# Moving a few on-chip tiles by 128 bytes, so that all matmul operands start at an odd multiple of 128

## The chip, the cores and the metric

The kernel runs on one core of one Trainium2 chip. The metric is the device time of one execution in microseconds (us). Three runs of the kernel before took 561.51, 562.34 and 562.51; the median is 562.34.

## The reference

Eight batches of 256 rows and 1024 features, in float32. Cross attention over a context of the same size, then a linear layer with 4-bit weights, both with a layer norm ahead and a residual behind:

```
def _L0_xattn_ref(text, features, Wq, bq, Wk, bk):
    Q = einsum('btx,dx->btd', text, Wq) + bq
    K = einsum('bpx,dx->bpd', features, Wk) + bk
    scores = einsum('btd,bpd->btp', Q, K) / sqrt(1024)
    attn = softmax(scores, axis=-1)
    return einsum('btp,bpd->btd', attn, features)

def _L0_ffn_ref(x, qweight, qzeros, scales, bias, g_idx):
    zeros = 4-bit fields of qzeros, + 1
    w = 4-bit fields of qweight
    wbin = where(w > 0, 1, -1)
    weights = scales[g_idx] * (wbin - zeros[g_idx])
    return x @ weights + bias

x = x + _L0_xattn_ref(layernorm(x), ctx, Wq, bq, Wk, bk)
x = x + _L0_ffn_ref(layernorm(x), qweight, qzeros, scales, bias, g_idx)
```

## The kernel before

The kernel keeps float32 accuracy with a fast matmul type: each operand is split into a high part (a rounded copy, made by ScalarE) and a low part (what is left, made by VectorE or GpSimd), and each product is three matmuls into the same accumulator: high by high, high by low, low by high. The helper is `three` (lines 1234 to 1237); in a matmul the first operand is the stationary one (128x128, loaded as weights) and the second the moving one (512 columns, in the scores 256). Line 1235 is high by high, 1236 has the low moving operand, 1237 the low stationary operand.

There are four stages on TensorE, in this order.

1. Projection (`proj`, lines 1262 to 1289). M = Wq' Wk, a 1024x1024 matrix, so that the scores are x M ctx'. Stationary wq_hi, wq_lo; moving wk_hi (line 1279), wk_lo (1282), wk_hi again with wq_lo (1285). 64 blocks (b, c) of two halves of three matmuls, 384 in all. The transposes of the first x tiles stand between the last blocks.
2. t products (lines 1340 to 1362). t = M' x' in four pairs of batches: for each pair p and each column block j, 24 matmuls (8 row blocks i by three), stationary m_hi and m_lo, moving xT_hi and xT_lo. 32 groups, 768 matmuls. The groups are counted n = 8p + j. After some of them stand gather steps (`gather`, two matmuls each, lines 1320 and 1321), which look up the scales and zeros of the 4-bit weights; VectorE makes the weights from them (`pick`, `weights`), and a layer norm and transposes of the next x run beside them.
3. Scores and attention products, batch by batch (`scores`, `pv`). The scores of one batch are 48 matmuls of 256 columns, stationary tT_hi and tT_lo, moving cT_hi and cT_lo. The attention product is 24 matmuls of 512 columns, stationary pT, moving cn.
4. The linear layer (`product`), as a seven-product scheme over halves: for each of eight batches (a pass) seven products a11, a12, s2, s1, s3, s4, a22 of 12 matmuls each (4 blocks k by three). Stationary l_hi and l_lo, moving r_tile0 to 2 for k = 0 to 2 and r_last for k = 3.

The order on each engine is written out by hand, with semaphores between engines. Tiles lie at places that are written out too: `at(name, kb, ...)` puts a tile at the byte `16512 + kb * 1024` of every partition (lines 76 to 79). Places are reused from stage to stage. Those that the change touches:

- WKL (line 102) holds wk_lo in stage 1 and xT_lo in stage 2, 32 KB from 98.125.
- tT_hi0, tT_hi1 (line 159) at 98.125 and 106.125; tT_hi2, used for batch 0 alone, is at 194.25.
- slot 6 and 7 (line 125), 8 KB each from 114.125: the t results and tT_lo of batches 6 and 7, the residual rows xres6 and xres7, and the unpacked weights and right sums of blocks 1 and 2 or 0 to 2.
- r_last2 (line 169), moving operand of the last two products' last block (s4 and a22), at 106.125.
- l_hi and l_lo of s2 and s1 (lines 178 to 180) at 98.125 and 102.125, the low part 2 KB behind the high.

16512 is 129 times 128. All other tiles of large matmuls are at whole KB or at a quarter of one, and so begin at an odd multiple of 128 bytes; those in the list begin at an even multiple.

Of the kernel before, what the change touches and what calls it, by code (L numbers as in the profile page):

```python
# [9 lines left out]
F32R = mybir.dt.float32r  # L10
# [3 lines left out]
P = 128  # L14
HALF = 512
# [33 lines left out]
def xattn_ffn_kernel(nc, x, ctx, Wq, bq, Wk, bk, qweight, qzeros, scales, bias, g_idx, out):  # L49
    B, S, D = x.shape  # L50
    G = scales.shape[0]
    assert ctx.shape == x.shape and S == 2 * P and D == 2 * HALF and bq.shape[0] == D
    NB = D // P
# [17 lines left out]
    with ExitStack() as stack:  # L71
# [6 lines left out]
        def at(name, kb, shape, dt):  # L78
            return nc.alloc_sbuf_tensor_at(name, shape, dt, offset=BASE + int(kb * KB)).ap()
# [19 lines left out]

        m_hi = at("m_hi", 2, [P, NB, D], F32R)  # L100
        m_lo = at("m_lo", 34, [P, NB, D], F32R)
        WKL = 98.125
        wk_hi = at("wk_hi", 66, [P, NB, D], F32R)
        wk_lo = at("wk_lo", WKL, [P, NB, D], F32R)

# [16 lines left out]
        xT_hi = at("xT_hi", 66, [P, NB, 2 * S], F32R)  # L122
        xT_lo = at("xT_lo", WKL, [P, NB, 2 * S], F32R)

        slot = [kb + 8 * i for kb in (130.25, 146.25, 82, 114.125) for i in range(2)]
        t_pair = [at(f"t_pair{p}", slot[2 * p], [P, 2, NB, S], F32) for p in range(PAIRS)]


# [21 lines left out]
        s3 = at("s3", 188.25, [P, D], BF16)  # L150
# [5 lines left out]
        cn_lo = at("cn_lo", 186.25, [P, QT, D], F32R)  # L156
        cT_hi = [at(f"cT_hi{i}", kb, [P, NB, S], F32R) for i, kb in enumerate((178.25, 66))]
        cT_lo = [at(f"cT_lo{i}", kb, [P, NB, S], F32R) for i, kb in enumerate((186.25, 74))]
        tT_hi = [at(f"tT_hi{i}", kb, [P, NB, S], F32R) for i, kb in enumerate((98.125, 106.125, 194.25))]
        tT_lo = [at(f"tT_lo{b}", slot[b], [P, NB, S], F32R) for b in range(B)]  # L160
        cin = [at(f"cin{i}", kb, [P, QT, D], F32) for i, kb in enumerate((162.25, 170.25, 58))]
        xres = [at(f"xres{b}", slot[b], [P, QT, D], F32) for b in range(B)]
# [3 lines left out]


        r_tile = [at(f"r_tile{k}", kb, [P, 2 * N_PROD, HALF], F32R) for k, kb in enumerate((2, 30, slot[0]))]
        r_last = [at(f"r_last{i}", kb, [P, m, HALF], F32R) for i, (kb, m) in enumerate(((slot[0] + 28, 2), (66, 8), (106.125, 4)))]

        def right(k, m):
            if k < KH - 1:
# [2 lines left out]
            return r_last[i][:, m - first, :]  # L175


        l_place = dict(a11=162.25, a12=166.25, s2=98.125, s1=102.125, s4=170.25, s3=174.25, a22=178.25)
        l_hi = {n: at(f"l_hi_{n}", kb, [P, HALF], F32R) for n, kb in l_place.items()}
        l_lo = {n: at(f"l_lo_{n}", kb + 2, [P, HALF], F32R) for n, kb in l_place.items()}  # L180
        l_sum = {n: at(f"l_sum_{n}", l_place[n] + 2, [P, HALF], F32) for n in ("s1", "s2", "s3", "s4")}
# [1311 lines left out]
```

## Time and profile before

| | us |
|---|---|
| median of three runs | 562.34 |
| profiled execution | 563.15 |
| its span | 561.4 |
| TensorE busy | 553.5 (99%) |
| VectorE busy | 386.2 (69%) |
| ScalarE busy | 240.4 (43%) |
| GpSimd busy | 186.2 (33%) |

The profile is of one execution. The span is from the first to the last instruction; 1.8 us of the execution lie around it. TensorE's weight loads are a row of their own and overlap its matmuls. A matmul's duration in the profile is the time from its start to its end, and the next one starts before that end.

### The profile page before, as it was taken

To read this page: it belongs to the slowest core of one execution; us is meant where nothing else is said; L and a number is where in the kernel's file an instruction comes from. 1 tells how busy PE (TensorE), PEld (TensorE's weight loads), DVE (VectorE), ACT (ScalarE), POOL (GpSimd) and SP (SyncE) were. 2 spreads that over 40 slices of the span, in tenths; PEclk is the share of its full clock that TensorE was granted. 3 is DMA by queue.
4 is the path that set the end of the run, shared out by engine and by line. 5 is a ranking of instruction groups with operands and counts; after the bars stand their busy time and mean duration, and the time that the engine had idled before them with its cause. 6 is when DMAs were issued, how large, how long until landed. Compare 5 with 4: busy or idle time off the path is not lost.

```text
span 561.4 us, 7445 instructions
## 1 busy us (share of the span) xinstructions
PE 553.5 (99%) x2702; PEld 456.5 (81%) x2702; DVE 386.2 (69%) x643; ACT 240.4 (43%) x426; POOL 186.2 (33%) x143
## 2 busy tenths in 40 slices
PE   7999999999999999999999999999999999999997
PEld 5888888887777877877889999999788888888886
DVE  4976765689889997785213555574877788778742
ACT  6964354301522342242336766676473253234110
POOL 2072000000000000000115977776667545743630
PEclk9999999999999999999999999999999999999999
DMA  8852100249576844743436699997517776773411
GB/s 287 252 156 70 37 1 0 90 172 311 177 224 238 251 188 150 223 160 131 156 99 245 231 340 354 313 402 308 228 76 224 226 218 231 216 233 110 118 75 75
DMA packets 47187, 106.59 MB, mean 190 GB/s; under 512 B 3576, under 2 KB 24064, under 8 KB 44976
## 3 DMA queue, kind: packets, MB, share of 16 engines
q1 hardware_dynamic: 40624, 99.84, 50.6%
q10 hardware_dynamic: 6528, 6.29, 5.0%
q8 instruction: 21, 0.34, 0.3%
q14 instruction: 14, 0.11, 0.1%
HBM read 66.27 MB, written 39.85 MB: 189 GB/s over the span
## 4 chain that ended last, share of the span: by engine, by line
PE 86%; DVE 5%; ACT 4%; DMA 2%; issue 2%; POOL 1%; SPq 0%; ACTq 0%; DVEq 0%; POOLq 0%
PE bank L1235 22%; PE bank L1237 22%; PE bank L1236 21%; PE bank L1279 5%; PE bank L1282 5%; PE bank L1285 5%; PE bank L1337 2%; DMA right_scratch<-part_hi 1%; DMA wk_stage<-in_L_xattn_Wk 1%; ACT yin L789 1%; POOL cn_lo L537 1%; PE bank L1245 1%; ACT cn_hi L586 1%; PE bank L1320 1%; DVE junk L1001 0%
## 5 line engine op out<-in xcount | busy, mean ns | idle before, releaser
L1235 PE MATMUL bank<-xT_hi,m_hi 128*128 128x512 f32 x256 | 104.5, 408 | 0.2 <-DVE xT_lo L853 0.2
L1237 PE MATMUL bank<-xT_hi,m_lo 128*128 128x512 f32 x256 | 100.8, 394 | 0.0
L1236 PE MATMUL bank<-xT_lo,m_hi 128*128 128x512 f32 x256 | 100.6, 393 | 0.0
L745 ACT ACTIVATE t_pair<-bank,ucol 128x512 f32<-128x512 f32 x32 | 22.0, 687 | 110.1 <-PE bank L1237 110.0
L1187 DVE TENSOR_TENSOR xres<-xres,bank 128x512 f32<-128x512 f32 x56 | 38.2, 682 | 36.9 <-PE bank L1237 36.8
L544 POOL TENSOR_TENSOR tT_lo<-t_pair,tT_hi 128x1024 fp32r<-128x1024 f32 x16 | 38.2, 2403 | 76.5 <-ACT tT_hi L586 76.5
L523 POOL TENSOR_TENSOR pairs<-mv,pairs 128x2 f32<-128x2 f32 x8 | 5.5, 693 | 164.4 <-DVE mv L920 164.4
L558 POOL TENSOR_TENSOR l_lo_s<-l_sum_s,l_hi_s 128x512 fp32r<-128x512 f32 x32 | 40.4, 1294 | 57.1 <-DVE l_sum_s L1128 57.1
L1235 PEld LDWEIGHTS bank<-xT_hi,m_hi 128*128 128x128 f32 x256 | 48.1, 188 | 13.1 <-DVE xT_lo L853 0.6
L1237 PEld LDWEIGHTS bank<-xT_hi,m_lo 128*128 128x128 f32 x256 | 48.1, 188 | 11.2
L1236 PEld LDWEIGHTS bank<-xT_lo,m_hi 128*128 128x128 f32 x256 | 48.2, 188 | 10.9 <-issue 0.2
L1279 PE MATMUL bank<-wk_hi,wq_hi 128*128 128x512 f32 x128 | 51.5, 403 | 1.5 <-ACT wk_hi L586 0.8
L1282 PE MATMUL bank<-wk_lo,wq_hi 128*128 128x512 f32 x128 | 50.7, 396 | 0.2 <-DVE wk_lo L862 0.2
L1285 PE MATMUL bank<-wk_hi,wq_lo 128*128 128x512 f32 x128 | 50.2, 392 | 0.0
L537 POOL TENSOR_TENSOR cn_lo<-cin,cn_hi 128x512 fp32r<-128x512 f32 x32 | 40.3, 1290 | 26.8 <-ACT cn_hi L586 26.8
L853 DVE TENSOR_TENSOR cT_lo<-bank,cT_hi 128x512 fp32r<-128x512 f32 x32 | 20.6, 686 | 34.1 <-ACT cT_hi L586 33.9
L564 POOL TENSOR_TENSOR xres<-xres,bias_rows 128x1024 f32<-128x1024 f32 x16 | 38.4, 2412 | 0.0
L1235 PE MATMUL bank<-r_tile,l_hi_s 128*128 128x512 f32 x96 | 37.7, 393 | 0.0
L1237 PE MATMUL bank<-r_tile,l_lo_s 128*128 128x512 f32 x96 | 37.7, 393 | 0.0
L1236 PE MATMUL bank<-r_tile,l_hi_s 128*128 128x512 f32 x96 | 37.7, 392 | 0.0
L1235 PE MATMUL bank<-cT_hi,tT_hi 128*128 128x256 f32 x128 | 37.0, 289 | 0.0
L1237 PE MATMUL bank<-cT_hi,tT_lo 128*128 128x256 f32 x128 | 36.1, 282 | 0.0
(148 smaller groups left out, 1257.2 us busy)
## 6 DMA issues: line engine op xcount, KB each, us to landing
cin<-in_ctx SPq DMA_DIRECT2D x8, 1024.0 KB, 5.5
xres<-in_x SPq DMA_DIRECT2D x8, 1024.0 KB, 11.2
out<-xres SPq DMA_DIRECT2D x15, 512.0 KB, 5.7
right_scratch<-part_hi SPq DMA_DIRECT2D x28, 256.0 KB, 2.2
xn_scratch<-xin SPq DMA_DIRECT2D x6, 1024.0 KB, 4.9
xq<-xn_scratch ACTq DMA_DIRECT2D x24, 256.0 KB, 5.5
r_tile<-right_scratch SPq DMA_DIRECT2D x6, 1024.0 KB, 11.0
yn_scratch<-yin SPq DMA_DIRECT2D x6, 1024.0 KB, 4.4
```

Of the source, the lines that this page charges most:

```text
L537: pool.tensor_tensor(cn_lo[:, kt, cols], cin[b % 3][:, kt, cols], cn_hi[:, kt, cols].bitcast(F32), ALU.subtract).then_inc(s_cnlo, 1)
L544: pool.tensor_tensor(tT_lo[b][:, ks, :], t_pair[b // 2][:, b % 2, ks, :], tT_hi[b % 2 if b else 2][:, ks, :].bitcast(F32), ALU.subtract).t ...
L558: pool.tensor_tensor(l_lo[name], l_sum[name], l_hi[name].bitcast(F32), ALU.subtract).then_inc(s_llo_p, 1)
L564: pool.tensor_tensor(x1_of(f)[:, t, :], x1_of(f)[:, t, :], bias_rows, ALU.add).then_inc(s_rb, 1)
L745: act.activation(t_pair[p][:, :, j, :], bank[n % 4][:, :].rearrange("p (b q) -> p b q", b=2), ACT.Identity, bias=ucol[:, j:j + 1]).then_in ...
L1187: dve.tensor_tensor(part, part, prod_bank(f, n)[:, :], ALU.add).then_inc(s_acc, 1)
L1235: pe.matmul(out_, a_hi, b_hi, start=start, stop=False, skip_group_check=True)
L1236: pe.matmul(out_, a_hi, b_lo, start=False, stop=False, skip_group_check=True)
L1237: return pe.matmul(out_, a_lo, b_hi, start=False, stop=stop, skip_group_check=True)
L1279: pe.matmul(out_, q_hi, wk_hi[:, c, cols], start=c == 0, stop=False, skip_group_check=True)
L1282: pe.matmul(out_, q_hi, wk_lo[:, c, cols], start=False, stop=False, skip_group_check=True)
L1285: ins = pe.matmul(out_, q_lo, wk_hi[:, c, cols], start=False, stop=c == NB - 1, skip_group_check=True)
```

## The change

Four numbers and what is built from them go down by 0.125 KB: 98.125 to 98, 102.125 to 102, 106.125 to 106 and 114.125 to 114. The tiles keep their sizes, and 128 bytes that lay free between 98 and 98.125 now lie free between the last moved tile and 130.25. No instruction is added, removed or moved on any engine.

```
-        WKL = 98.125
+        WKL = 98
...
-        slot = [kb + 8 * i for kb in (130.25, 146.25, 82, 114.125) for i in range(2)]
+        slot = [kb + 8 * i for kb in (130.25, 146.25, 82, 114) for i in range(2)]
...
-        tT_hi = [at(f"tT_hi{i}", kb, [P, NB, S], F32R) for i, kb in enumerate((98.125, 106.125, 194.25))]
+        tT_hi = [at(f"tT_hi{i}", kb, [P, NB, S], F32R) for i, kb in enumerate((98, 106, 194.25))]
...
-        r_last = [at(f"r_last{i}", kb, [P, m, HALF], F32R) for i, (kb, m) in enumerate(((slot[0] + 28, 2), (66, 8), (106.125, 4)))]
+        r_last = [at(f"r_last{i}", kb, [P, m, HALF], F32R) for i, (kb, m) in enumerate(((slot[0] + 28, 2), (66, 8), (106, 4)))]
...
-        l_place = dict(a11=162.25, a12=166.25, s2=98.125, s1=102.125, s4=170.25, s3=174.25, a22=178.25)
+        l_place = dict(a11=162.25, a12=166.25, s2=98, s1=102, s4=170.25, s3=174.25, a22=178.25)
```

## Rows read from the trace of the kernel before

**Rows 1.** Page, part 1: busy us (share of the span) and instructions, TensorE.
```profile
PE 553.5 (99%) x2702; PEld 456.5 (81%) x2702; DVE 386.2 (69%) x643; ACT 240.4 (43%) x426; POOL 186.2 (33%) x143
```
**Rows 2.** Windows: stretch, PE, PEld, DVE, ACT, POOL busy (x), clock, DMA, GB/s.
```profile
12.60:103.60 91.00, 91.00 (x418) 74.16 (x418) 66.24 (x92) 51.13 (x113) 14.61 (x10) 1.00 0.27 86
104.80:292.90 188.10, 187.47 (x818) 147.77 (x817) 139.83 (x259) 55.54 (x93) 8.94 (x8) 1.00 0.58 190
292.90:407.50 114.60, 113.78 (x764) 103.57 (x763) 63.32 (x109) 74.75 (x143) 81.77 (x54) 1.00 0.80 299
407.50:558.00 150.50, 150.50 (x665) 123.23 (x663) 109.90 (x176) 50.87 (x71) 77.01 (x57) 1.00 0.51 164
```
**Rows 3.** Timeline (start us, us, engine, line), last attention product: first and 24th matmul.
```profile
401.97 0.39 PE L1235 MATMUL bank<-cn_hi,pT_hi 128*128 128x512 f32 x1
...
407.18 0.40 PE L1237 MATMUL bank<-cn_hi,pT_lo 128*128 128x512 f32 x1
```
**Rows 4.** Timeline, projection: a matmul and the 48th behind it.
```profile
42.04 0.40 PE L1279 MATMUL bank<-wk_hi,wq_hi 128*128 128x512 f32 x1
...
53.24 0.40 PE L1279 MATMUL bank<-wk_hi,wq_hi 128*128 128x512 f32 x1
```
**Rows 5.** Timeline, t products: starts of neighbouring groups of 24, at three places.
```profile
110.77 0.40 PE L1235 MATMUL bank<-xT_hi,m_hi 128*128 128x512 f32 x1
...
116.37 0.40 PE L1235 MATMUL bank<-xT_hi,m_hi 128*128 128x512 f32 x1
...
187.25 0.39 PE L1235 MATMUL bank<-xT_hi,m_hi 128*128 128x512 f32 x1
...
192.74 0.39 PE L1235 MATMUL bank<-xT_hi,m_hi 128*128 128x512 f32 x1
...
263.40 0.40 PE L1235 MATMUL bank<-xT_hi,m_hi 128*128 128x512 f32 x1
...
268.95 0.40 PE L1235 MATMUL bank<-xT_hi,m_hi 128*128 128x512 f32 x1
```
**Rows 6.** Timeline, linear layer: starts of products a11, a12, s2, s3, s4, next a11.
```profile
461.56 0.39 PE L1235 MATMUL bank<-r_tile,l_hi_a 128*128 128x512 f32 x1
...
464.31 0.39 PE L1235 MATMUL bank<-r_tile,l_hi_a 128*128 128x512 f32 x1
...
467.04 0.40 PE L1235 MATMUL bank<-r_tile,l_hi_s 128*128 128x512 f32 x1
...
472.62 0.39 PE L1235 MATMUL bank<-r_tile,l_hi_s 128*128 128x512 f32 x1
...
475.36 0.39 PE L1235 MATMUL bank<-r_tile,l_hi_s 128*128 128x512 f32 x1
...
480.85 0.39 PE L1235 MATMUL bank<-r_tile,l_hi_a 128*128 128x512 f32 x1
```
**Rows 7.** Timeline, scores: 12 matmuls of batch 0, then 12 of batch 2.
```profile
294.41 0.28 PE L1235 MATMUL bank<-cT_hi,tT_hi 128*128 128x256 f32 x1
...
295.85 0.38 PE L1337 MATMUL bank<-ident,cin 128*128 128x128 f32 x2
...
315.11 0.28 PE L1235 MATMUL bank<-cT_hi,tT_hi 128*128 128x256 f32 x1
...
316.53 0.28 PE L1235 MATMUL bank<-cT_hi,tT_hi 128*128 128x256 f32 x1
```
**Rows 8.** Chain that ended last, 104 to 205: start us, us, what.
```profile
151.96 0.63 ACT xT_hi L586
...
181.31 0.39 PE bank L1320
...
202.72 0.50 PE bank L1235
```
**Rows 9.** DMA issues near 448 and 487: count, KB, us to landing.
```profile
xres<-x_scratch SPq DMA_DIRECT2D x1, 1024.0 KB, 4.8
...
xres<-x_scratch SPq DMA_DIRECT2D x1, 1024.0 KB, 4.6
```

## The prediction

> **What bounds the kernel now.** I read the busy shares first, then the stretches, then the starts of single matmuls in the timeline, and last the chain of waits. TensorE is busy 553.5 us of a 561.4 us span [rows 1], at full granted clock in all four stretches [rows 2], and in each it is busy for nearly the whole stretch: 91.00 of 91.00, 187.47 of 188.10, 113.78 of 114.60, 150.50 of 150.50 [rows 2]. So the end moves with the distance from the start of one matmul to the start of the next, which I call the step. The duration in a row (0.39 to 0.40) is no help: it is longer than the step, because matmuls overlap. The step must be taken from starts, over many matmuls, since a row is rounded to 0.01.
>
> **What the steps say.** The base is 16512 bytes, 129 times 128. A place in whole KB or with .25 behind it is therefore an odd multiple of 128, a place with .125 an even one. Only the places at 98.125 to 122.125 are even now. The change makes no instruction more or fewer and moves none; if it does anything, it does it through the step. Four comparisons:
>
> - The last attention product (rows of batch 7: cn and pT, all operands odd) starts its matmuls at 401.97 and its 24th at 407.18 [rows 3]: 5.21/23 = 0.2265, say 0.2267 with the half nanoseconds that rounding hides (12 matmuls are 2.72). This is my odd step.
> - The projection has wk_lo at an even place as the moving operand of every third matmul: 48 matmuls from 42.04 to 53.24 [rows 4], 11.20/48 = 0.2333.
> - The t products have xT_lo at an even place, also every third. One group of 24 takes 5.60 at the start (110.77 to 116.37), 5.49 in the middle (187.25 to 192.74), 5.55 late (263.40 to 268.95) [rows 5]: steps of 0.2333, 0.2288 and 0.2313. With the odd step it would be 5.44.
> - In the last stage, seven products of 12 matmuls, all in one pass of 19.29 (461.56 to 480.85) [rows 6]. a12, all odd, takes 2.73 (464.31 to 467.04). s2 and s1, whose stationary operands are at 98.125 and 102.125, take 5.58 for 24 (467.04 to 472.62), 2.79 each. s3 takes 2.74, and s4 and a22, three of whose twelve moving operands are at 106.125, 5.49 for 24 (475.36 to 480.85). a11, which follows such a product, takes 2.75.
>
> The last stage weighs most: same line, same shape, same engines beside it, and 2.79 against 2.73 goes with the place alone. It also shows that a product with every operand odd is still a little long just after a mixed one (2.74, 2.75) and then comes down to 2.73. The even operand need not be the moving one.
>
> **The change part by part.**
>
> 1. Projection (WKL, 98.125 to 98). 384 matmuls, 3 times 128. The first 18 wait for loads (until 12.6, the first stretch that isn't in rows 2), and what follows them gains; 366 x (0.2333 - 0.2267) = 2.4. Beside the x transposes of the last block a few steps are long for another reason; I take off 0.1: **2.3**.
> 2. t products (xT_lo, same place). 768 matmuls, 32 groups of 24, in which the two of each gather step are not counted. Seven groups go at 5.60 (five first, two last), three at 5.49, 22 at 5.55: 7 x 0.16 + 3 x 0.05 + 22 x 0.11 = 3.7. Not all of this reaches the end. The chain leaves TensorE for ScalarE at 151.96, goes on through VectorE's weights, sums, splits and row terms, and comes back at the gather at 181.31; and it comes back again at 202.72, when VectorE has made the last two blocks of xT_lo [rows 8]. Those stretches hang on work that isn't shortened. TensorE gets there earlier and waits: of the groups 8 to 12 I lose 5 x 0.11, of 16 and 17 0.05 + 0.11 (the gather near 210 is fed by the same unbroken run of VectorE), 0.7 in all. Left 3.0; I take **2.9**, since some other gather may come late too. Cover elsewhere: VectorE is busy 139.83 of 188.10 in this stage [rows 2], so it has room on the mean.
> 3. Scores (tT_hi at 98.125 and 106.125 for batches 1 to 7; tT_lo in the moved slots for 6 and 7). Here the rows go the other way. Batch 0, all odd, has 12 matmuls of 256 columns from 294.41 to 295.85, 1.44; batch 2, tT_hi even, has 12 from 315.11 to 316.53, 1.42 [rows 7]. Over 48 such matmuls in each of five batches (1 to 5) that would be 240/12 x 0.02 = 0.4; just behind the transposes both batches go alike, so I take half, **-0.2**. For 6 and 7 both are even now, and I put no loss.
> 4. Attention products. All their operands are odd before and after: 0.
> 5. Last stage (l_hi and l_lo of s1, s2; r_last of the last two products). 19.29 now, 84 x 0.2267 = 19.04 after: 0.25 a pass, 2.0 for eight; the first pass has waits in its first products, so **1.9**. VectorE has 109.90 of 150.50 busy [rows 2] and keeps up.
> 6. The other tiles at 114.125 (t_pair3, xres6 and xres7, some weights and sums of the right side). But for tT_lo they are no matmul's operand. What they might cost is in their transfers. The load of xres5 (at an odd place) takes 4.8 to land, that of xres7 (even now) 4.6 [rows 9], 1 MB each. If the place did that, it would cost 0.2 on a few loads that nothing waits for at their end: 0.
>
> The Trainium skill ("DMA: Bandwidth & Descriptors", How a descriptor splits into AXI transactions) speaks against the change here: a transfer whose start isn't at a multiple of 256 bytes fetches from the boundary below, so that a 4 KB row would cost 132 beats in place of 128. By that rule the moved loads would take 3% longer, an estimate of 0.14 on 4.7; by the rows a difference as small as this can neither be seen nor ruled out, and in the sum both give 0, because these loads are far ahead of their readers.
>
> Sum: 2.3 + 2.9 - 0.2 + 1.9 = **6.9 us**. The profiled execution took 563.15 in all, 1.8 of it around its span, and would take 556.2. It lies 0.8 above the median of the runs, 562.34; the gain set against that gives **555.4**.
>
> **Rivals.**
>
> A. The place is only half of it. For: the t products go at three rates with the same places, so the step also depends on how the reads stand to each other in time, and each rate holds for many groups until something disturbs it. An all-odd stage could settle at a rate such as 0.2288 [rows 5]. Against: every all-odd stretch of 512 columns comes down to 0.2267, after each disturbance. At 0.2288: projection 366 x 0.0045 = 1.6; t products 7 x 0.11 + 22 x 0.06 = 2.1, less 0.4 in VectorE's stretches, 1.7; last stage 1.9; scores -0.2. Gain 5.0, time 557.3.
>
> B. Nothing happens: 562.3. The steps would come from the kind of operand (split parts, tiles of another stage, other engines' reads) and not from its place. For: the projection's first matmul of three, with two odd operands, is as slow as the others. Against: a12 and s2 differ in nothing else that I can see, and neighbours of an even operand share its cost in the last stage too. The Trainium skill ("TensorE: Matmul & The Clock Gate", Step-by-step: what each phase is for) would have it so: matrix unit reads go through two independent ports, and loading the next weights takes no bandwidth from the running matmul. By it a place could not matter; the 2.79 against 2.73 of this trace is what it leaves unexplained.
>
> C. Slower. Two streams that start at the same parity get into each other's way, as the scores hint: 1.44 against 1.42 is 1.4%. If the all-odd step of the first two stages, where xT and m stand in other relations than r_tile and l_hi, went that way, 366 + 768 = 1,134 matmuls of some 0.233 would cost 1.4% more: +3.7, with the scores' 0.2 the time is 566.2. It decides where the mean step of those stages comes out above 0.2325. Against: the all-odd rows of 512 columns are the fastest in the trace.
>
> D. TensorE outruns VectorE in the whole t stage up to its last gather at 257: another 7 x 0.11 = 0.8 is lost, 556.2. This lies inside the range.
>
> **How the numbers follow.** The forecast, with D in it, 0.76; A 0.12; B 0.07; C 0.05. The likeliest case alone spans 554.2 (nothing lost to VectorE and in the scores, 2.4 + 3.7 + 2.0 gained) to 556.6. The range goes up to 557.8 to take in A and leaves B and C out, and down to 554.0. What a measurement of this kernel can tell from no change is 0.2%, 1.1 us. Faster: forecast, A, and none of the others, 0.88. Same: B and a little of A and C, 0.08. Slower 0.04.
>
> **What would show it.** Right: groups of 24 t matmuls of 5.44; 48 projection matmuls in 10.88; a pass of the last stage in 19.04, with s1 and s2 at 2.72; scores of batch 2 at 1.44 for 12; TensorE's wait for the gather near 181 about 0.5 longer than its 0.4. Wrong: steps as before (B), a rate between (A), a projection above 0.2333 (C), or more waits of TensorE on VectorE than 1 us (step 2).

## The result and the profile after

The changed kernel takes 556.12 us (median of four runs, 555.50 to 556.69), the kernel before 561.92 beside it (561.22 to 562.51). The ratio is 0.9897, with a 95% interval of 0.9879 to 0.9915: 5.8 us or 1.0% faster. Forecast were 555.4 and a range of 554.0 to 557.8.

The page of the changed kernel, part 1 (busy us, share of the span, instructions), answers to [rows 1]; the span is 554.9.

```profile
PE 546.3 (98%) x2702; PEld 456.5 (82%) x2702; DVE 385.4 (69%) x643; ACT 239.1 (43%) x426; POOL 186.1 (34%) x143
```

The same instructions, the same weight loads to the tenth of a microsecond, and 7 us less of matmul. The four stages as stretches of the changed kernel, cut as in [rows 2] (the projection from its 19th matmul, the last stage from product s2 of the first pass; columns as there):

```profile
12.80:102.60 89.80, 89.80 (x420) 74.54 (x419) 67.78 (x94) 52.03 (x115) 14.61 (x10) 1.00 0.29 90
102.60:288.00 185.40, 184.37 (x818) 147.77 (x817) 139.80 (x260) 54.97 (x92) 8.93 (x8) 1.00 0.59 193
288.00:402.80 114.80, 114.03 (x763) 103.81 (x762) 63.30 (x109) 74.68 (x143) 81.72 (x54) 1.00 0.79 298
402.80:551.30 148.50, 148.50 (x665) 123.14 (x664) 108.83 (x176) 50.45 (x71) 77.02 (x57) 1.00 0.51 165
```

Granted clock and instructions are as before; counts differ by one or two where a cut falls. Taken between the same instructions in both traces (the 19th projection matmul, the first t product, the first score, product s2 of the first pass, the last matmul), the stages are:

| stage | before | after | forecast | measured |
|---|---|---|---|---|
| projection behind its first 18 matmuls | 92.12 | 89.86 | -2.3 | -2.26 |
| t products | 188.13 | 185.32 | -2.9 | -2.81 |
| scores, attention, first two products of the last stage | 114.52 | 114.83 | +0.2 | +0.31 |
| last stage from s2 of the first pass | 150.34 | 148.43 | -1.9 | -1.91 |

The first loads came 0.18 later in the profiled run of after, so the spans differ by 6.5. The timeline of the changed kernel (start us, us, engine, line): first a projection matmul and the 48th behind it, which were 11.20 apart [rows 4], then one t group, which was 5.60, 5.49 or 5.55 [rows 5]:

```profile
41.38 0.39 PE L1279 MATMUL bank<-wk_hi,wq_hi 128*128 128x512 f32 x1
...
52.26 0.39 PE L1279 MATMUL bank<-wk_hi,wq_hi 128*128 128x512 f32 x1
...
114.00 0.39 PE L1235 MATMUL bank<-xT_hi,m_hi 128*128 128x512 f32 x1
...
119.44 0.39 PE L1235 MATMUL bank<-xT_hi,m_hi 128*128 128x512 f32 x1
```

10.88 and 5.44: the odd step, 0.2267, in both. The pass of the last stage that [rows 6] show, in the changed kernel: a11, s2, s3, and the next a11.

```profile
456.30 0.39 PE L1235 MATMUL bank<-r_tile,l_hi_a 128*128 128x512 f32 x1
...
461.74 0.39 PE L1235 MATMUL bank<-r_tile,l_hi_s 128*128 128x512 f32 x1
...
467.18 0.39 PE L1235 MATMUL bank<-r_tile,l_hi_s 128*128 128x512 f32 x1
...
475.34 0.39 PE L1235 MATMUL bank<-r_tile,l_hi_a 128*128 128x512 f32 x1
```

The pass is 19.04 (19.29 before), s2 and s1 together 5.44 (5.58). The scores went the other way. The starts of batch 2 and batch 3 in the kernel before, then in the changed one:

```profile
314.75 0.29 PE L1235 MATMUL bank<-cT_hi,tT_hi 128*128 128x256 f32 x1
...
328.10 0.29 PE L1235 MATMUL bank<-cT_hi,tT_hi 128*128 128x256 f32 x1
```

```profile
309.86 0.28 PE L1235 MATMUL bank<-cT_hi,tT_hi 128*128 128x256 f32 x1
...
323.28 0.28 PE L1235 MATMUL bank<-cT_hi,tT_hi 128*128 128x256 f32 x1
```

13.42 a batch, 13.35 to 13.37 before. And TensorE waits longer for VectorE, at the gather that [rows 8] have at 181.31 and at the last blocks of xT_lo (202.72 there). Before, then in the changed kernel; the brackets give TensorE's idle time and what ended it:

```profile
180.49 0.40 PE L1237 MATMUL bank<-xT_hi,m_lo 128*128 128x512 f32 x1
181.31 0.39 PE L1320 MATMUL bank<-zz,onehot 72*128 72x512 bf16 x1 [0.43 <-DVE wt L1030]
...
202.13 0.39 PE L1237 MATMUL bank<-xT_hi,m_lo 128*128 128x512 f32 x1
202.72 0.50 PE L1235 MATMUL bank<-xT_hi,m_hi 128*128 128x512 f32 x1 [0.20 <-DVE xT_lo L853]
```

```profile
176.88 0.39 PE L1237 MATMUL bank<-xT_hi,m_lo 128*128 128x512 f32 x1
177.88 0.39 PE L1320 MATMUL bank<-zz,onehot 72*128 72x512 bf16 x1 [0.62 <-DVE wt L1030]
...
198.52 0.39 PE L1237 MATMUL bank<-xT_hi,m_lo 128*128 128x512 f32 x1
199.29 0.50 PE L1235 MATMUL bank<-xT_hi,m_hi 128*128 128x512 f32 x1 [0.38 <-DVE xT_lo L853]
```

The steps over these two waits were 0.82 and 0.59 and are 1.00 and 0.77; a step without a wait is 0.23. The two waits together grew from 0.63 to 1.00.

### The profile page after: what moved, and what is told of

Same layout as the page of the kernel before. It is cut to its first block, busy times and chain, and to the rows that moved or that the text cites. A ratio compares the mean times of both kernels' runs of the same rounds, so it can differ in the third digit from the quotient of the medians.

```text
span 554.9 us, 7445 instructions
## 1 busy us (share of the span) xinstructions
PE 546.3 (98%) x2702; PEld 456.5 (82%) x2702; DVE 385.4 (69%) x643; ACT 239.1 (43%) x426; POOL 186.1 (34%) x143
## 4 chain that ended last, share of the span: by engine, by line
PE 86%; DVE 5%; ACT 4%; DMA 2%; issue 2%; POOL 1%; SPq 0%; ACTq 0%; DVEq 0%; POOLq 0%
PE bank L1235 22%; PE bank L1237 22%; PE bank L1236 22%; PE bank L1279 5%; PE bank L1282 5%; PE bank L1285 5%; PE bank L1337 2%; DMA wk_stage<-in_L_xattn_Wk 1%; DMA right_scratch<-part_hi 1%; ACT yin L789 1%; POOL cn_lo L537 1%; PE bank L1245 1%; ACT cn_hi L586 1%; PE bank L1320 1%; DVE junk L1001 0%
```

## Experiments

The theory: the step (from the start of one matmul to the start of the next) of a 512-column matmul depends on where its moving and its stationary operand start, relative to each other; nothing else in the change acts. The rivals are told with each run. The runs with a median and an interval were timed against the kernel before; the others are one profile and one time.

### Each part alone

e1_wkl_only, a diff against the kernel before:

```
-        WKL = 98.125
+        WKL = 98
```

> Only WKL moved to 98 (wk_lo of the projection, xT_lo of the t products); everything else as before. Theory (the step depends on the place of the operands): the projection takes 10.88 for 48 matmuls, a group of 24 t products 5.44, and a pass of the last stage stays at 19.29. The comparison of the two profiles gave 2.1 for the projection and 2.8 for the t products, so about 4.9 of the gain: a ratio near 0.991, some 557.0. Rival (the moved places act through something they share, such as a wait or a transfer, and not one by one): the gain would not divide this way, and the last stage would change too or the first two would not.

Measured: 557.28, ratio 0.9923 (0.9908 to 0.9938). Its projection and its products s2 and s1:

```profile
51.96 0.39 PE L1279 MATMUL bank<-wk_hi,wq_hi 128*128 128x512 f32 x1
...
62.84 0.39 PE L1279 MATMUL bank<-wk_hi,wq_hi 128*128 128x512 f32 x1
...
461.44 0.40 PE L1235 MATMUL bank<-r_tile,l_hi_s 128*128 128x512 f32 x1
...
467.03 0.39 PE L1235 MATMUL bank<-r_tile,l_hi_s 128*128 128x512 f32 x1
```

10.88 and 5.59: fast where the tile moved, as before where it didn't.

e2_last_only, against the kernel before:

```
-enumerate(((slot[0] + 28, 2), (66, 8), (106.125, 4)))]
+enumerate(((slot[0] + 28, 2), (66, 8), (106, 4)))]
...
-s2=98.125, s1=102.125
+s2=98, s1=102
```

> Only the places of the last stage moved: l_hi and l_lo of s2 and s1 to 98 and 102, r_last2 to 106. Theory: passes of 19.04 in place of 19.29, first two stages as before, 1.9 less in all (ratio 0.9966, some 560.0). Rival (the early stages' gain is what shortens the end): no change, 561.9.

Measured: 559.38, ratio 0.9962 (0.9948 to 0.9976).

```profile
52.66 0.40 PE L1279 MATMUL bank<-wk_hi,wq_hi 128*128 128x512 f32 x1
...
63.76 0.40 PE L1279 MATMUL bank<-wk_hi,wq_hi 128*128 128x512 f32 x1
...
464.46 0.39 PE L1235 MATMUL bank<-r_tile,l_hi_s 128*128 128x512 f32 x1
...
469.90 0.39 PE L1235 MATMUL bank<-r_tile,l_hi_s 128*128 128x512 f32 x1
```

The mirror image: s2 and s1 in 5.44. The two ratios multiply to 0.9885, within the interval of the whole change; the parts add up. One thing was not as expected: the projection of this kernel took 11.10 and not 11.20, with the same places and the same program there. Its t products took 187.19, and not 188.13, for a part by the same cause (groups of 5.55 from the start, which before went at 5.60 there). A mixed stage can fall into more than one rate from one execution to the next. No stage whose tiles all agree did in any run: 10.88 and 5.44 each time.

### Odd, or only alike?

e3_all_even, against the changed kernel:

```
-        BASE = 16512
+        BASE = 16640
```

> The changed kernel with every tile of the core 128 bytes higher, so that every operand starts at an even multiple of 128 and all distances between tiles stay as in the changed kernel. Theory (only the places relative to each other count): the same as the changed kernel, 48 projection matmuls in 10.88, t groups of 5.44, passes of 19.04, about 556.1, ratio 0.990. Rival (an operand is slow because it starts at an even multiple): every stage of 512 columns slow, steps of 0.233 or more, 562 or above.

Measured: 556.01, ratio 0.990 (0.9885 to 0.9915), the same as the changed kernel.

```profile
52.16 0.39 PE L1279 MATMUL bank<-wk_hi,wq_hi 128*128 128x512 f32 x1
...
63.04 0.39 PE L1279 MATMUL bank<-wk_hi,wq_hi 128*128 128x512 f32 x1
...
461.19 0.39 PE L1235 MATMUL bank<-r_tile,l_hi_s 128*128 128x512 f32 x1
...
466.62 0.39 PE L1235 MATMUL bank<-r_tile,l_hi_s 128*128 128x512 f32 x1
```

10.88 and 5.43. An odd multiple of 128 has no merit; that all are alike does. The change's own words name the wrong half of its cause.

### Moving against stationary, or moving against the next moving?

e5_moving_even, against the changed kernel; only the projection's places count:

```
-        WKL = 98
-        wk_hi = at("wk_hi", 66, [P, NB, D], F32R)
+        WKL = 98.125
+        wk_hi = at("wk_hi", 66.125, [P, NB, D], F32R)
...
-        xT_lo = at("xT_lo", WKL, [P, NB, 2 * S], F32R)
+        xT_lo = at("xT_lo", 98.25, [P, NB, 2 * S], F32R)
...
-(130.25, 146.25, 82, 114)
+(130.25, 146.25, 82, 114.25)
```

> The changed kernel, but in the projection both moving tiles (wk_hi at 66.125, wk_lo at 98.125) are at even multiples of 128 and both stationary ones stay odd; xT_lo is at 98.25 and the slots from 114 at 114.25, all odd, so the later stages are as in the changed kernel. Theory M (moving against stationary: what counts is the parity of the moving stream against the weights read beside it): the projection is slow throughout, about 0.2325 a matmul as in the products s2 and s1 before, 48 matmuls in 11.16. Rival A (alternation: a matmul is slow when the next moving operand has another parity than its own): all moving operands are alike, so 10.88 as in the changed kernel.

Measured (one run): 557.19.

```profile
52.34 0.40 PE L1279 MATMUL bank<-wk_hi,wq_hi 128*128 128x512 f32 x1
...
63.49 0.40 PE L1279 MATMUL bank<-wk_hi,wq_hi 128*128 128x512 f32 x1
...
462.24 0.39 PE L1235 MATMUL bank<-r_tile,l_hi_s 128*128 128x512 f32 x1
...
467.68 0.39 PE L1235 MATMUL bank<-r_tile,l_hi_s 128*128 128x512 f32 x1
```

11.15 for 48, a step of 0.2323: slow, though all moving operands agree among themselves. So the place of the moving stream against the stationary operand costs by itself. It isn't the whole of it: if each matmul paid only for its own two operands, the projection of the kernel before, where one moving tile in three is off, would take about 10.97 (a third of the 0.27 added to 10.88), but took 11.20, and 11.10 in e2; and in the kernel before all three of its matmuls are slow (236, 234 and 230 ns at lines 1279, 1282 and 1285). A change of place from one matmul to the next seems to add to the cost; no run here tells how.

A weight load lies beside the matmul ahead of it. From the changed kernel:

```profile
42.06 0.39 PE L1279 MATMUL bank<-wk_hi,wq_hi 128*128 128x512 f32 x1
42.07 0.19 PEld L1282 LDWEIGHTS bank<-wk_lo,wq_hi 128*128 128x128 f32 x1
```

This makes a clash between the two reads the natural reading; no run here took the weight load away from a matmul, so this part is argued, not shown.

### The distance between the two

Five kernels with the same edit against the changed kernel, with o = 1/16, 1/32, 3/16, 7/32 and 3/32 KB in turn:

```
-        WKL = 98
+        WKL = 98 + o
...
-(98, 106, 194.25)
+(98 + o, 106 + o, 194.25)
...
-s2=98, s1=102
+s2=98 + o, s1=102 + o
...
-(130.25, 146.25, 82, 114)      and      (106, 4)
+(130.25, 146.25, 82, 114.25)   and      (106.25, 4)
```

> The changed kernel with wk_lo, xT_lo, tT_hi0 and 1, l_hi and l_lo of s2 and s1 64 bytes above the odd multiple of 128 (98.0625 and so on); r_last2 and the slots from 114 are at odd multiples. Theory G (address bit 7 of the two streams must agree): 64 bytes off is half agreement, so s2 and s1 take between 2.72 and 2.79, about 2.75, and the projection 48 in about 11.04. Rival Z (any distance that isn't a multiple of 256 costs the same): 2.79 and 11.20. Rival S (a finer structure, a distance exists that is better than none): below 2.72.

> As the run with 64 bytes, with 32 bytes (98.03125 and so on). Theory G (share of agreement of address bit 7): s2 and s1 2.74, 48 projection matmuls about 10.96. Rival Z (any distance costs the same): 2.79 and 11.20. Rival S: below 2.72.

> As the run with 64 bytes, with 192 bytes (98.1875 and so on), which is 64 bytes short of the next odd multiple. Theory G: as at 64 bytes, about 2.75 for s2 and s1, 11.04 for 48 projection matmuls. Rival Z: 2.79 and 11.20. Rival D (the sign of the distance counts, which stream runs ahead): clearly unlike the run with 64 bytes.

> As the runs with 64, 32 and 192 bytes, with 224 bytes (98.21875 and so on), 32 short of the next odd multiple. Those gave s2 and s1 2.80, 2.80 and 2.75 each, 48 projection matmuls 11.14, 11.20 and 10.99, and 1.41 to 1.42 for the first 12 scores of a batch. Theory D (the direction counts: a tile that starts somewhat below the next multiple costs less than one as far above): between 2.72 and 2.75, and 10.88 to 10.99. Rival F (only the distance to the nearest multiple of 256 counts, and 192 was mild by chance of the moment): like 32 bytes, 2.80 and 11.20.

> The same with 96 bytes (98.09375 and so on). Theory D: like 64 and 128 bytes, 2.79 to 2.80 and 11.1 to 11.2. Rival F: like the two neighbours as well; for a nearest-distance rule in which 64 and 192 differ by chance anything from 2.74 to 2.80. The scores' 12 matmuls lie between those at 64 bytes (1.413) and at 128 (1.426).

Rows of the products s2 and s1 (start of s2, start of s3) at 64 bytes, then at 192:

```profile
465.74 0.40 PE L1235 MATMUL bank<-r_tile,l_hi_s 128*128 128x512 f32 x1
...
471.34 0.39 PE L1235 MATMUL bank<-r_tile,l_hi_s 128*128 128x512 f32 x1
```

```profile
462.35 0.39 PE L1235 MATMUL bank<-r_tile,l_hi_s 128*128 128x512 f32 x1
...
467.85 0.39 PE L1235 MATMUL bank<-r_tile,l_hi_s 128*128 128x512 f32 x1
```

All of them, read from starts in the same way. The row at 0 is the changed kernel, that at 128 the kernel before, which has r_last2 and the slots from 114 at even multiples too; their times are medians of four, the other times are single runs. In the products s2 and s1 and in the scores it is the stationary tile that was moved, in the projection one moving tile in three.

| bytes above the odd multiple | s2 and s1, 24 matmuls | 48 of the projection | first 12 scores of batch 3 | time |
|---|---|---|---|---|
| 0 | 5.44 | 10.88 | 1.432 | 556.12 |
| 32 | 5.59 | 11.20 | 1.424 | 562.71 |
| 64 | 5.60 | 11.14 | 1.413 | 561.62 |
| 96 | 5.61 | 11.09 | 1.440 | 561.60 |
| 128 | 5.59 | 11.20 | 1.425 | 561.92 |
| 192 | 5.50 | 10.99 | 1.414 | 557.59 |
| 224 | 5.60 | 11.20 | 1.413 | 561.88 |

The idea that half an agreement costs half fell: 32 bytes cost as much as 128. So did the idea that a tile just short of the next multiple is cheap: 224 bytes cost as much as 32. What stands is that for 512 columns every distance tried that isn't a whole multiple of 256 costs, six out of six, and that 192 costs about half of what the others do, or less. Why 192 is mild is open. It isn't the signed distance of the moving tile from the stationary one alone: that sign is opposite in s2 and s1 and in the projection, so that 192 in one would be 64 in the other, and yet 192 is mild and 64 isn't in both. For 256 columns zero is nearly the worst place, and 64, 192 and 224 are the best. The scores at 96 bytes missed what was expected, between 1.413 and 1.426: they took 1.440, the slowest of all.

### The scores, and a place that is better for them

e4_scores_even, against the changed kernel:

```
-(130.25, 146.25, 82, 114)
+(130.25, 146.25, 82, 114.25)
...
-(98, 106, 194.25)
+(98.125, 106.125, 194.25)
```

> The changed kernel, but tT_hi of batches 1 to 7 at an even multiple of 128 (98.125 and 106.125), and the slots from 114 at 114.25, odd as well, so that the scores mix parities and all else is odd. Theory (a matmul of 256 columns is a little faster when they mix): the scores of batches 2 to 5 take 5.78 again in place of 5.83, those of 6 and 7 too, all in all 0.3 to 0.4 less than the changed kernel: some 555.8 by the median, to be seen in the profile rather than in the time. Rival (the scores' difference is chance of the moment, set by what stands before them): batches stay at 5.83.

Measured: 555.78, ratio 0.9893 (0.9878 to 0.9908). Batch 2 to 3:

```profile
309.35 0.29 PE L1235 MATMUL bank<-cT_hi,tT_hi 128*128 128x256 f32 x1
...
322.72 0.29 PE L1235 MATMUL bank<-cT_hi,tT_hi 128*128 128x256 f32 x1
```

13.35 to 13.37 in place of 13.42, also from batch 6 to 7. The scores' loss is their tile's place and nothing else.

e11_scores64 and e12_scores224 are the same edit with (98.0625, 106.0625, 194.25) and (98.21875, 106.21875, 194.25).

> The changed kernel with tT_hi of batches 1 to 7 at 98.0625 and 106.0625, 64 bytes above an odd multiple, and the slots from 114 at 114.25; everything that 512-column matmuls read stays odd. From the 64-byte run the scores of a batch with what stands between them are 0.085 shorter than in the changed kernel, times seven is 0.6: 555.3 beside 556.0, ratio to before about 0.9885. Theory (the step depends on the places of the two tiles alone): 12 scores in 1.413 in each batch, t groups 5.44, passes 19.04. Rival (the gain in the scores is given back in the attention products behind them, or by waits): 556.

> As the run that has tT_hi of batches 1 to 7 at 64 bytes above an odd multiple of 128, with 224 bytes (98.21875 and 106.21875). In the run where all moved tiles were at 224 bytes the scores of a batch with what stands between them took 6.95, beside 6.97 to 6.98 at 64 bytes and 7.06 in the changed kernel. Theory (places alone): 6.95 again, 12 scores in 1.413, all 512-column stages as in the changed kernel; 0.8 less than the changed kernel, 555.2 to 555.3, which its time alone can't tell from 555.5. Rival (what stands around the scores made the difference): 6.97 to 7.06.

Batch 2 to 3 at 64 bytes, then at 224:

```profile
309.64 0.28 PE L1235 MATMUL bank<-cT_hi,tT_hi 128*128 128x256 f32 x1
...
322.95 0.28 PE L1235 MATMUL bank<-cT_hi,tT_hi 128*128 128x256 f32 x1
```

```profile
309.67 0.28 PE L1235 MATMUL bank<-cT_hi,tT_hi 128*128 128x256 f32 x1
...
322.98 0.28 PE L1235 MATMUL bank<-cT_hi,tT_hi 128*128 128x256 f32 x1
```

13.31 in both. The times are 555.54, ratio 0.9890 (0.9873 to 0.9906), and 555.55, ratio 0.9880 (0.9863 to 0.9896). Both medians lie 0.6 below the changed kernel's, and the stage of scores and attention takes 114.25 and 114.20 in place of 114.83; but the intervals overlap, and the t products of these two profiles took 0.3 more than the changed kernel's. That they beat the kernel before is shown; that the stage of the scores is 0.6 shorter is shown by the profiles; that the whole kernel beats the changed one isn't shown.

## Why the prediction was right

The forecast 555.4 against 556.12. By its steps:

1. Projection: 2.3 forecast, 2.26 measured, the step 0.2267 as taken from an all-odd stretch of another stage. Run e1 shows it alone.
2. t products: 2.9 and 2.81. The groups went to 5.44. The loss to VectorE came in the places named, but not with the sizes named: the wait for the gather near 181 was to grow by 0.5 and grew by 0.2, from 0.43 to 0.62. Between the start of group 8 and the gather at 181.31 (177.88 after), before took 29.88 and after 29.59, where none was forecast to be gained. From that gather to the one at 210.32 (206.89) it is 29.01 in both: nothing gained. It is 28.99 to 29.03 in all other runs too but three with slow places, e2, e6 and e7, which took 28.92, 28.86 and 28.89: this stretch goes by VectorE's chain and not by the step. From there to the scores 82.58 became 81.11, as the steps give.
   The first of these stretches is where executions differ. It took 28.81 in e4, where TensorE did not wait for the gather, and 29.89 in e11, where the step over the gather was 1.26; with the old places 29.29 in e2 without the wait, 29.88 in the profile of before with it. So VectorE's chain comes late here or not, by up to 1.1 us from one execution to the next (why it varies isn't shown), and the gain in this stretch lies between nothing and 0.5. Over all profiles with the places of after in this stage (e1, e3, e4, e5, e11, e12 and after: 184.5 to 185.6, mean 185.1) against the two with the old ones (188.13 and 187.19) the mean gain is 2.6, not 2.8.
3. Scores: 0.2 forecast, 0.3 measured. The scores of a batch from 2 to 5, with what stands between them, took 7.00 and take 7.06; those of 6 and 7 took 7.04 and take 7.06. The direction and the step were right (1.43 for the first 12 scores of batch 2, where 1.44 was forecast); the term was too small because I halved the 0.4 that the rows gave and put nothing for batches 6 and 7.
4. Attention products: nothing, and their settling steps changed by a hundredth or two.
5. Last stage: 1.9 and 1.91. Run e2 shows it alone.
6. Transfers: nothing seen. The 1 MB loads of the last stage take 4.7 to 4.8 in the changed kernel, wherever they land, 4.6 to 4.8 before [rows 9]. Run e3 is the better test: there all four of these loads start at a multiple of 256 bytes and take 4.73, 4.68, 4.79 and 4.75; in the changed kernel none does, and they take 4.75, 4.72, 4.80 and 4.75, 0.02 more on the mean. By the Trainium skill ("DMA: Bandwidth & Descriptors", How a descriptor splits into AXI transactions) they would take 0.14 longer, by the estimate of the prediction; these loads don't show that.

What is left of the difference, 6.9 forecast and 5.8 measured in the medians: the stages sum to 6.67 in the pair of profiles, less 0.18 at the first loads, 6.5. The profiled run of before, 563.15, was 1.2 above the median of its runs, and its share of the wait on VectorE was among the longest; that of after, 556.69, lay 0.6 above its own. The sum was made against a slow member of the family. That can be put in numbers, as an estimate from only two executions with the old places, the profiles of before and e2: their projection took 92.12 and 91.36, their t products 188.13 and 187.19. Against the means of the two, the changed places gain 1.9 and 2.6, and with 0.3 lost and 1.9 gained behind them 6.1 in all, near the 5.8 of the medians; the first two alone make 4.5, and e1, which has only these, measured 4.4. So the mechanism and the direction of each term were right, but that 2.26 and 2.81 came out so near to 2.3 and 2.9 was partly luck: both were read from, and measured against, the same slow execution of the kernel before.

Of the rivals, A (an all-odd stage settles at a slower rate) fell: each group came down to 5.44 and 10.88. B (the place does nothing) fell with e1 and e2. The rule named with it, of the Trainium skill ("TensorE: Matmul & The Clock Gate", Step-by-step: what each phase is for), that loading the next weights takes nothing from the running matmul, would have the places without effect; e5 and e3 don't bear this out, 0.2323 against 0.2267 a matmul by the places of the two operands alone. Whether the weight load is what collides is the open part told above. C (same parities clash) has only the scores for it, at the 0.3 us that they weigh. D (TensorE outruns VectorE up to 257) fell behind 210; what VectorE's chain withheld ahead of it, about 0.2 up to the gather at 181 and 0.4 from there to 210, is near the 0.7 of step 2, otherwise divided.

One argument of the prediction was weaker than it looked. It spoke of odd and even, with all-odd as the only state that the trace had to show. The same rows would have fitted "alike" as well as "odd", and e3 shows that it is alike.

## What to carry to other kernels

Where TensorE is the bound and its matmuls follow each other without a gap, measure the step from start to start over many matmuls and hold it against the same shape elsewhere in the trace: a difference of 2.5 to 3% at the same clock was the places of the operands here. For 512 columns of this type start moving and stationary tiles at a multiple of 256 bytes from each other, which was the fastest of the seven distances tried; for 256 columns 64 or 224 bytes off was better by up to 2%. And a gain in the step reaches the end only where no other engine's chain runs through the stretch: here two of the four stages gave it whole, and one gave nothing over 29 us.

## What the runs showed of the hardware that was not expected

- With the operands alike, the step is 226.7 ns for 512 columns and 120.0 for 256. At 2.4 GHz, the full granted clock that these stretches show, that is 544 and 288 cycles: the columns and 32 more. No distance tried brought 512 columns below it; for 256 columns 64, 192 and 224 bytes gave 117.8 ns over the first twelve scores of a batch, where distance 0 gave 119.3.
- A mixed stage has several steady rates with the same places and program: 5.60, 5.55 and 5.49 for a t group in one execution, 11.20 and 11.10 for 48 projection matmuls in two. It keeps a rate until a wait or another kind of matmul disturbs it.
- After a wait, a gather or a run of transposes even an all-alike stretch needs some more matmuls before it is back at 226.7: in the changed kernel 2 behind the gather at 177.88 (232 and 231 ns), 10 in the attention product of batch 2 (224 to 236 ns, down and up).
